# A graph layer with gathered rows: ScalarE takes a chunk's sums earlier, TensorE's own product stands behind slot 3, and one queue writes the factor pieces

## The reference, cut to what matters

```
def _cheb_norm(src, dst, n):
    deg = segment_sum(ones, src, n)
    dinv = where(deg > 0, rsqrt(maximum(deg, 1.0)), 0.0)
    return -dinv[src] * dinv[dst]

def _cheb_conv(x, src, dst, norm, W0, W1, b):
    tx1 = segment_sum(x[src] * norm[:, None], dst, n)
    return x @ W0 + tx1 @ W1 + b

h   = maximum(layernorm(x), 0.0)
h   = _cheb_conv(h, src, dst, norm, W1_0, W1_1, b1)
h   = layer_norm(h, gamma, beta)
h   = where(h >= 0, h, 0.01 * h)
out = x + _cheb_conv(h, src, dst, norm, W2_0, W2_1, b2)
```

## Time and profile before

| | |
|---|---|
| median of 3 runs | 2129.64 us (2129.09 to 2132.87) |
| the profiled execution | 2125.4 us, with a span of 2123.5 us |
| busy share | PE 89%, ACT 71%, POOL 70%, DVE 69%, PEld 50% |
| DMA | 515.61 MB, 243 GB/s on average |
| chain that ended last | POOL 33%, PE 22%, "issue" 15%, ACT 13%, DMA 11%, DVE 5% |
| gathers | 1564, 948 ns each |

### The profile page before, as it was taken

The page is one execution under the profiler, slowest core; times in us unless marked ns, Lnnn a source line. Parts: engine busy times, 40 slices in busy tenths (PEclk is TensorE's granted clock), DMA queues, the critical chain, the costliest instruction groups (busy, mean ns, idle before and its releaser), DMA issues.

```text
span 2123.5 us, 25622 instructions
## 1 busy us (share of the span) xinstructions
PE 1900.1 (89%) x6702; PEld 1067.5 (50%) x6702; DVE 1457.6 (69%) x3379; ACT 1509.1 (71%) x2720; POOL 1487.0 (70%) x1574
## 2 busy tenths in 40 slices
PE   3459999999999999999996999999999999999998
PEld 3325555555555555555543555555555555555554
DVE  9948777777777777777765555556565655666653
ACT  7757777778777777787755666666666666666664
POOL 0067777777777777777746777777777777777774
PEclk9979999999999999999997999999999999999999
DMA  9998888888888888888856888888888888888885
GB/s 230 284 297 241 239 239 242 241 241 238 242 242 241 238 241 242 241 236 242 241 149 217 250 255 255 254 246 254 252 250 255 254 255 251 252 253 246 256 254 158
DMA packets 195466, 515.61 MB, mean 243 GB/s; under 512 B 44312, under 2 KB 45999, under 8 KB 195325
## 3 DMA queue, kind: packets, MB, share of 16 engines
q0 software_dynamic: 125120, 411.69, 65.9%
q1 hardware_dynamic: 67376, 101.91, 15.3%
q10 hardware_dynamic: 2828, 0.44, 0.1%
HBM read 473.08 MB, written 40.84 MB: 242 GB/s over the span
## 4 chain that ended last, share of the span: by engine, by line
POOL 33%; PE 22%; issue 15%; ACT 13%; DMA 11%; DVE 5%; SPq 0%; ACTq 0%; POOLq 0%; DVEq 0%
POOL arena L494 33%; PE ps L1093 12%; DMA arena<-table,idx_all 10%; PE ps L1230 5%; ACT ps L597 3%; ACT high L597 3%; PE ps L1223 2%; PE ps L1221 2%; DVE low L918 1%; ACT hots_full L549 1%; ACT high L598 1%; ACT arena L630 1%; ACT arena L536 1%; ACT arena L555 1%; DVE ps L1000 1%
## 5 line engine op out<-in xcount | busy, mean ns | idle before, releaser
L494 POOL DMA_INDIRECT arena<-table,idx_all x1564 | 1483.2, 948 | 549.7 <-issue 499.6
L922 DVE TENSOR_TENSOR low<-arena,ps 128x512 fp32r<-128x512 f32 x517 | 353.4, 686 | 391.6 <-ACT ps L598 378.8
L1221 PE MATMUL ps<-high,hots 128*128 128x512 f32 x1034 | 569.8, 551 | 4.6 <-ACT high L597 2.4
L1230 PE MATMUL ps<-arena,hots_full 128*128 128x512 f32 x1060 | 544.6, 596 | 0.4 <-DMA arena<-table,idx_all 0.4
L918 DVE SCALAR_TENSOR_TENSOR low<-arena,ps 128x512 fp32r<-128x512 f32 x517 | 385.8, 747 | 209.8 <-ACT ps L597 177.8
L598 ACT CAST ps<-arena 128x512 fp32r<-128x512 f32 x517 | 304.3, 589 | 315.0 <-DMA arena<-table,idx_all 307.6
L1223 PE MATMUL ps<-low,hots 128*128 128x512 f32 x1034 | 408.4, 395 | 0.0
L597 ACT ACTIVATE ps<-arena 128x512 fp32r<-128x512 f32 x517 | 354.3, 685 | 45.3 <-DMA arena<-table,idx_all 45.1
L597 ACT ACTIVATE high<-arena 128x512 fp32r<-128x512 f32 x517 | 369.6, 715 | 0.0
L598 ACT CAST high<-arena 128x512 fp32r<-128x512 f32 x517 | 317.8, 615 | 1.4 <-PE ps L1223 1.4
L892 DVE TENSOR_SCALAR hots<-iota_f,loc_all 128x128 fp32r<-128x128 f32 x1034 | 264.8, 303 | 9.8 <-PE ps L1223 6.1
(11 more groups left out here) (133 smaller groups left out, 1330.9 us busy)
## 6 DMA issues: line engine op xcount, KB each, us to landing
arena<-table SPq DMA_DIRECT2D x106, 256.0 KB, 3.7
arena<-table,idx_all POOLq DMA_INDIRECT x1564, 3.9
table<-arena SPq DMA_DIRECT2D x53, 256.0 KB, 4.0
arena<-in_x_dram SPq DMA_DIRECT2D x53, 256.0 KB, 6.0
out_dram<-arena SPq DMA_DIRECT2D x53, 256.0 KB, 3.9
table<-arena SPq DMA_DIRECT2D x10, 1120.0 KB
arena<-in_x_dram SPq DMA_DIRECT2D x9, 1120.0 KB
w_all<-in_L_gnn_W_dram SPq DMA_DIRECT2D x2, 1024.0 KB, 9.9
```

The source lines that it names most:

```text
L494: nc.gpsimd.indirect_dma_start(out=rows[u][:, c, 0:RW if L == 0 else D], out_offset=None, in_=table[L][:, :], in_offset=bass.IndirectOffse ...
L922: nc.vector.tensor_tensor(low[a], rows[u][:, c, 0:D], high_ps[s % NB][:, :], ALU.subtract).then_inc(s_low, 1)
L1221: nc.tensor.matmul(tx_ps[u][:, :], hot, high[a], start=c == 0, stop=False)
L1230: last = nc.tensor.matmul(tx_ps[u][:, :], hot, rows[u][:, c, 0:D], start=c == 0, stop=i == NC - 2 and c == SLOTS - 1)
```

## The change

It has four parts.

1. **Sums.** ACT's `take_tx` of chunk i - 1 stands behind two high parts of chunk i instead of six. `copy_txT` stands behind four instead of eight.
2. **PE.** `transpose_tx` stands behind slot 3 instead of slot 4. `dense_own` of chunk i comes directly behind it instead of between slots 13 and 14. `dense_tx` stands behind slot 5 instead of slot 7.
3. **Norm.** In layer 0 the norm's first steps (`conv_stats`, `take_std`, `norm1`) of chunk i - 1 are done in chunk i, where before it was two chunks later. `make_sloped` and `finish1` stay two chunks later, but earlier in the chunk. In layer 1 `finish2` comes one chunk later instead of two. The one-hots of the next chunk are made in other portions.
4. **Prologue.** ACT's queue writes all factor pieces, and SP's none. The transfer of `dst` in rows stands behind the table's on SP. DVE does the order check and the chunk bases ahead of the node scales. PE turns the `dst` rows after the two small matmuls. POOL's wait for the table stands in the layer instead of ahead of the branch.

The diff, cut to its core:

```diff
@@ sync @@
-            slot_rows(dst, dst_rows, s_dsts)
             for g in range(1, NG):
...
-            sp.wait_ge(s_factor, 1)
-            with nc.allow_non_contiguous_dma(reason="the factor in each row of the table"):
-                for n0, n1 in ((ACT_ROWS, TA), (TA, TR)):
-                    sp.dma_start(table_rows[n0:n1, :, D:RW], factors[n0:n1, :, :]).then_inc(s_factor_out, 16)
+            slot_rows(dst, dst_rows, s_dsts)
@@ gpsimd @@
-            pool.wait_ge(s_tab, 2 * 16 * (NG - 1))
-            pool.wait_ge(s_factor_out, 48)
...
+                else:
+                    pool.wait_ge(s_tab, 2 * 16 * (NG - 1))
+                    pool.wait_ge(s_factor_out, 32)
@@ scalar @@
-                act.dma_start(table[0].rearrange("(p t) n -> p t n", t=NT)[0:ACT_ROWS, :, D:RW],
-                              factors[0:ACT_ROWS, :, :]).then_inc(s_factor_out, 16)
+                for n0, n1 in ((0, TA), (TA, TR)):
+                    act.dma_start(table[0].rearrange("(p t) n -> p t n", t=NT)[n0:n1, :, D:RW],
+                                  factors[n0:n1, :, :]).then_inc(s_factor_out, 16)
...
-                    highs(0, 4)
-                    if L == 0 and i >= 2:
-                        take_std(i - 2)
-                    highs(4, 5)
+                    highs(0, 1)
                     if L == 0 and i >= 2:
                         make_sloped(i - 2, u)
-                    highs(5, 6)
-                    copy_own(L, i, u)
+                    highs(1, 2)
                     if i >= 1:
                         take_tx(L, i - 1, 1 - u)
-                    highs(6, 8)
+                    copy_own(L, i, u)
+                    highs(2, 4)
                     if i >= 1:
                         copy_txT(L, i - 1)
-                    highs(8, NS)
+                    highs(4, 9)
+                    if L == 0 and i >= 1:
+                        take_std(i - 1)
+                    highs(9, NS)
@@ vector, dve_step @@
-                    lows(0, 4)
-                    factor_hots(L, i, u, h, (4, 5))
-                    if i >= 2:
-                        if L == 0:
-                            epi = conv_stats(i - 2, u)
-                        else:
-                            finish2(i - 2, u, h - 1)
...
+                    lows(7, 8)
+                    factor_hots(L, i, u, h, (11,))
+                    if i >= 1:
+                        if L == 0:
+                            epi = conv_stats(i - 1, 1 - u)
+                        else:
+                            finish2(i - 1, 1 - u, (i - 1) // 2)
                     lows(8, 9)
+                    factor_hots(L, i, u, h, (13,))
                     if i <= NC - 3:
                         nc.vector.tensor_scalar(hotx_of(u), iota_f[:, :], col(loc_next, i), None,
                                                 ALU.is_equal).then_inc(s_hotx, 1)
+                    if L == 0 and i >= 1:
+                        norm1(i - 1, 1 - u, epi)
                     lows(9, 10)
@@ tensor, step @@
-                    slots(i, u, h, 0, 5)
+                    slots(i, u, h, 0, 4)
                     if i >= 1:
                         transpose_tx(L, i - 1)
-                    slots(i, u, h, 5, 8)
+                    dense_own(L, i, u)
+                    slots(i, u, h, 4, 6)
                     if i >= 1:
                         dense_tx(L, i - 1, 1 - u)
-                    slots(i, u, h, 8, 11)
+                    slots(i, u, h, 6, 11)
                     if i <= NC - 2:
                         transpose_own(L, i + 1, 1 - u, h + u)
-                    slots(i, u, h, 11, 14)
-                    if i < NC - 1:
-                        dense_own(L, i, u)
-                    slots(i, u, h, 14, SLOTS)
+                    slots(i, u, h, 11, SLOTS)
```

More of the change, by code:

```diff
@@ L42, in gnn_kernel @@
     TA = 112
-    ACT_ROWS = 48
     XG = (0, 2) + tuple(range(5, NT + 1, 5))
@@ L832, in _ @@
             nc.vector.reciprocal(factors[:, :, 0], sqrt_veps_deg).then_inc(s_factor, 1)
+            dve.wait_ge(s_idxps, 1)
+            nc.vector.tensor_copy(idx_all[:, 0:4 * P], src_ps[0][:, :]).then_inc(s_idxr, 1)
+            nc.vector.tensor_copy(idx_all[:, 4 * P:S], src_ps[1][:, 0:S - 4 * P]).then_inc(s_idxr, 1)
+            order()
+            bases()
             post.add(nc.vector.tensor_scalar(hasdeg, hist_ps[0:TR, 0:NT], 0.0, None, ALU.is_gt))
@@ L846, in _ @@
             dve.sem_inc(s_scales, 1)
-            dve.wait_ge(s_idxps, 1)
-            nc.vector.tensor_copy(idx_all[:, 0:4 * P], src_ps[0][:, :]).then_inc(s_idxr, 1)
-            nc.vector.tensor_copy(idx_all[:, 4 * P:S], src_ps[1][:, 0:S - 4 * P]).then_inc(s_idxr, 1)
             dve.wait_ge(s_dsts, 48)
@@ L855, in _ @@
                                   dst_rows[0:S - FB * P, FB * P:]).then_inc(s_dstrows, 1)
-            order()
-            bases()
             dve.wait_ge(s_locps, 1)
@@ L1032, in next_hots @@
                             hots_of(L, i + 1, c0, c1)
-                    lows(0, 4)
-                    factor_hots(L, i, u, h, (4, 5))
-                    if i >= 2:
-                        if L == 0:
-                            epi = conv_stats(i - 2, u)
-                        else:
-                            finish2(i - 2, u, h - 1)
-                    lows(4, 5)
-                    if L == 0 and i >= 2:
-                        norm1(i - 2, u, epi)
-                    lows(5, 6)
-                    factor_hots(L, i, u, h, (8,))
+                    lows(0, 2)
                     if L == 0 and i >= 2:
                         finish1(i - 2, u)
+                    lows(2, 4)
+                    factor_hots(L, i, u, h, (4, 5))
+                    hots_of(L, i, 10, SLOTS)
                     if more and (L or i):
@@ L1051, in dve_step @@
                     next_hots(0, 3)
+                    lows(4, 6)
+                    factor_hots(L, i, u, h, (8,))
+                    next_hots(3, 7)
                     lows(6, 7)
-                    next_hots(3, 5)
+                    next_hots(7, 10)
                     lows(7, 8)
-                    factor_hots(L, i, u, h, (11, 13))
-                    next_hots(5, 10)
+                    factor_hots(L, i, u, h, (11,))
+                    if i >= 1:
+                        if L == 0:
+                            epi = conv_stats(i - 1, 1 - u)
+                        else:
+                            finish2(i - 1, 1 - u, (i - 1) // 2)
                     lows(8, 9)
+                    factor_hots(L, i, u, h, (13,))
                     if i <= NC - 3:
@@ L1060, in dve_step @@
                                                 ALU.is_equal).then_inc(s_hotx, 1)
+                    if L == 0 and i >= 1:
+                        norm1(i - 1, 1 - u, epi)
                     lows(9, 10)
-                    next_hots(10, SLOTS)
                 if L:
                     dve.wait_ge(s_slot, summed(L, -1, SLOTS))
-                hots_of(L, 0, 0, SLOTS)
+                hots_of(L, 0, 0, 10)
                 chunks_of(dve_step)
-                for i in (NC - 2, NC - 1):
-                    if L == 0:
-                        norm1(i, i % 2, conv_stats(i, i % 2))
-                        finish1(i, i % 2)
-                    else:
-                        finish2(i, i % 2, i // 2)
+                if L == 0:
+                    finish1(NC - 2, 1)
+                    norm1(NC - 1, 0, conv_stats(NC - 1, 0))
+                    finish1(NC - 1, 0)
+                else:
+                    finish2(NC - 1, 0, (NC - 1) // 2)
             with dve.If(bad > 0):
@@ L1121, in _ @@
                              stop=True).then_inc(s_histend, 1)
-            pe.wait_ge(s_dstrows, 2)
-            turn(dst_ps, dst_rows_f).then_inc(s_locps, 1)
             pe.wait_ge(s_viol, 1)
@@ L1130, in _ @@
                              stop=True).then_inc(s_basesum, 1)
+            pe.wait_ge(s_dstrows, 2)
+            turn(dst_ps, dst_rows_f).then_inc(s_locps, 1)
             pe.wait_ge(s_flag, 1)
```

1 line of the change is left out of this document (removed).

## The result

| | before | changed |
|---|---|---|
| median | 2129.36 us (2128.14 to 2132.87, 4 runs) | 2328.89 us (2323.60 to 2334.24, 4 runs) |
| span of the profiled execution | 2123.5 us | 2324.6 us |
| mean granted clock | 0.982 | 0.957 |

The changed kernel takes 1.0939 times the time of the one before, with a 95% interval of [1.0924, 1.0954]. The forecast was 2260 us, so 69 us are missing from it, and the time lies outside the range.

A forecast was written before the change was run, and what follows sets the result against it. POOL's gathers, 18.5 us a mean chunk, were taken as the bound, to be overtaken by both layers' rings. +126 - 2.4 + 7 = +131 on 2125.4 gave 2256, plus 4.2 for the median: 2260 us, range 2225 to 2290.

The forecast's parts named there:

- the two rings: Per-chunk cycles of waits between ACT, DVE and PE: 20.2 us in layer 0, 19.5 in layer 1, against the gathers' 18.5.
- layer 0's ring, up to the first gather of layer 1: Layer 0's cycle through the norm, 52 turns of 20.2 us; layer 1 starts at 1205.5 instead of 1121.24, +84 us.
- layer 1's ring and end: Layer 1's cycle through the sums, 52 turns of 19.4 us, then 10.0 us to the end; +126 us with layer 0.
- clock: PE's products at half clock after its waits: four cases of 1.7 us, +7 us; possibly none, or 178 in every chunk.
- prologue: Factor transfers on ACT's queue alone, ahead of the first gather: a gain between 0 and 8.4 us, taken as 2.4.
- The gathers as the bound, and a ring that overtakes them: POOL's gathers pace both layers at 18.5 us a chunk; the new order's cycles take 20.2 and 19.4 us.
- ACT's place closes the ring: PE's transposes wait for ACT's take_tx, copy_own and high parts of slots 2 and 3; layer 1's link is 4.24 us.
- The rival in which the clock falls regularly: PE at half clock in a third of the chunks: 60 us instead of 7, thus 2313 us; chance 0.09.
- The signs named ahead: POOL waits on PE over 1 us, L620 waits in most chunks, PE share about 85%, gap between layers over 28.11 us.

The follow-up runs named there:

- the kernel with zeros: The changed kernel with four matmuls by zeros, adding nothing, in PE's wait ahead of slot 2: 2259.36 us, 1.0584 times the kernel before.

## Why the prediction was wrong

The sign, the mechanism and the two rings were right; the sum missed by two terms. Against the span of before, with the clock's part read off the kernel with zeros:

| term | forecast | measured |
|---|---|---|
| layer 0's ring, up to the first gather of layer 1 | +84 | 1217.7 - 1121.2 less 13.6 of its prologue: +82.9 |
| layer 1's ring and end | +42 | (2257.7 - 1217.7) - (2123.5 - 1121.2): +37.7 |
| clock | +7 | what is left, 201.1 - 10.0 - 82.9 - 37.7: +70.5 |
| prologue | -2.4 | 123.6 - 113.6: +10.0 |
| sum | +131 | +201.1 |

- **The gathers as the bound, and a ring that overtakes them:** shown. The turns that no half-clock stretch touched are 20.1 us in layer 0, forecast 20.2; and 19.4 and, after a short chunk, 19.0 in layer 1, forecast 19.5 and 19.04. With the half-clock stretches the mean turns were 20.6 and 20.3 us. That 2259 us of the kernel with zeros comes so near to the forecast of 2260 is partly luck, since its prologue was 13.6 us longer.
- **ACT's place closes the ring:** shown for layer 1, where it alone gave back everything. For layer 0 the forecast had the norm in the ring. The waits of the changed kernel bear this out, with 50 waits of ACT for the variance and one for the sums; no experiment at the shorter level took it apart. The forecast led this ring through `norm1` and line 648, where ACT waited in 14 turns only. In the others ACT came last by its own order, from line 642 on.
- **The clock is the step that failed.** The forecast put it so: "I count four such cases, +7 us". There were 50. The price of one was about right, 70.5 / 50 = 1.4 us against 1.7: (1233.9 - 123.6) - (1217.7 - 127.2) = 19.8 us for the 20 up to layer 1, and 50.7 us, 1.7 each, for the 30 of layer 1. What failed was the count, and the reason is in the forecast's own text: it had found a half-clock stretch behind a wait of 2.12 us, it had worked out a new wait in every chunk, and it still took the few cases of the old trace for the rule. In the new trace the wait is 1.61 us in one piece and 0.49 more, and in half of all turns the clock fell in it or behind it. The Trainium skill, "TensorE: Matmul & The Clock Gate", section "HAM oscillation — how this bites in real kernels", tells of a kernel whose matmuls stand still for a transfer between bursts, so that every burst starts slow. By that rule every turn here would have a slow stretch; the trace agrees in 50 of 104. The rival in which the clock falls regularly had 0.09; its 2313 us, with the prologue's 12 us more, are 2325, near the result.
- **The prologue was on the wrong side.** The forecast bounded it between a gain of 8.4 and nothing, because SP's 8.37 us went away. It did not ask what the queue does to which the rows go: two queues had shared them, and one then took 22.59 us. A cost was left out of the bounds, not just mis-sized.
- **The signs named ahead** came as named but for one: POOL's waits for PE, single ones up to 3.8 us; L630 in nearly every chunk; PE ahead of slots 2 and 3; PE's share 87% for 85; a gap of 46.80 us for 28.11. L620's waits were not in most chunks of both layers: 51 of the 52 on line 1166 are in layer 1.

## What to carry to other kernels

When a step that others wait for is moved forward in an engine's order, look at what it is moved in front of: here two casts that the next engine needed before it could use the result, and the ring went from 15.5 us, by the forecast's sum, to 20.1 and 19.4 us as measured. When a change makes TensorE wait in every iteration, price the half clock for a large share of the iterations, not for the few cases of a trace in which it hardly waited; a few matmuls by zeros in the wait can show what it costs, as they did here on one occasion. When transfers of short rows move to another queue, their time on that queue needs a price of its own.

## What the runs showed of the hardware

- Work that adds nothing made the kernel 70 us shorter. In the changed kernel, half of the turns of 20 us had a stretch at granted clock 0.50 that began in a wait of 1.5 to 1.6 us or close behind it; with 0.8 us of bf16 matmuls in this wait, three stretches were left in the whole run.
- The occasions differ more than any change here. On four of them the kernel before took 1.16 to 1.19 times as long, the changed kernel 1.21 times (2814.97 against 2328.89), and the kernel with zeros 1.24 times (2802.33 against 2259.36). By the record one and the same chip gave 2129.69 us and, five minutes later, 2473.32 us for the kernel before, so the level is not a property of the chip. Gathers that didn't wait still followed each other at 1.25 us, and casts took what they took elsewhere. The granted clock of the kernel before was 0.91 to 0.93 there, for 0.98 to 0.99. But in the kernel with the new prologue alone, which is no slower than the one before, there were new waits, whose releaser the profile can't name:

```profile
ACT arena L630 <- remote: 188.1, 37, 7.7
POOL arena L495 <- remote: 148.7, 49, 6.8
DVE ps L983 <- remote: 96.1, 36, 3.2
```

What makes them was not found.
